# x plus attention output moved from VectorE in the attention loop to GpSimd in the dense loop, through stored parts

## The reference

```
x2  = x + tanh(g_xattn) * autocorrelation(layernorm(x), ctx, ctx)
n   = layernorm(x2)
out = x2 + tanh(g_ffn) * (n @ W_base.T + b_base + moe(n))
moe: h = n @ A_w (8 experts x 16), gate from softmax(n @ W_gate.T) - threshold, (h * gate) @ B_w * 2
```

## Time and profile before

| | |
|---|---|
| three runs | 3029.5, 3030.46, 3032.73 us; median 3030.46 us |
| profiled execution | 3031.29 us, its span 3029.5 us |
| mean granted clock of TensorE | 0.990 |
| PE busy | 2921.9 us, 96% |
| DVE, ACT, POOL busy | 1606.0, 1012.6, 1454.0 us |
| HBM read, written | 223.76 MB, 67.21 MB |

### The profile page before, as it was taken

How to read it: one execution, slowest core, us unless ns; L and a number is a source line. 1 busy time by engine, 2 the same in 40 slices (tenths; PEclk the granted TensorE clock), 3 DMA queues, 4 the chain that set the end, 5 groups by cost and what they waited for, 6 DMA issues and landing times.

```text
span 3029.5 us, 37059 instructions
## 1 busy us (share of the span) xinstructions
PE 2921.9 (96%) x13184; PEld 1466.0 (48%) x13184; DVE 1606.0 (53%) x2738; ACT 1012.6 (33%) x1672; POOL 1454.0 (48%) x577
## 2 busy tenths in 40 slices
PE   4999999999999999997799999999999999999999
PEld 2445554555545554553644444444444444444444
DVE  3899989999999999998722121121211112111111
ACT  4555556555555545441511121111211112111110
POOL 4788888889888888884031211212112121221210
PEclk8999999999999999999899999999999999999999
DMA  8455544555455554423634132331323313233230
GB/s 201 124 123 126 139 110 118 127 132 125 115 122 125 135 117 102 101 73 111 237 98 111 56 111 75 91 111 55 111 72 94 106 60 111 69 97 99 68 97 28
DMA packets 260355, 324.49 MB, mean 107 GB/s; under 512 B 162911, under 2 KB 163487, under 8 KB 245541
## 3 DMA queue, kind: packets, MB, share of 16 engines
q1 hardware_dynamic: 259922, 323.38, 40.1%
q10 hardware_dynamic: 348, 0.18, 0.0%
HBM read 223.76 MB, written 67.21 MB: 96 GB/s over the span
## 4 chain that ended last, share of the span: by engine, by line
PE 84%; DVE 5%; POOL 3%; issue 2%; DMA 2%; ACT 1%; SPq 1%; ACTq 0%; DVEq 0%; POOLq 0%
PE bank L1097 43%; PE bank L488 7%; PE bank L422 7%; PE bank L454 6%; PE bank L472 5%; PE bank L460 3%; POOL spec_o L869 3%; DVE rows_mem L1256 2%; PE bank L1086 1%; PE bank L1087 1%; PE bank L1088 1%; ACT wt L548 1%; PE bank L435 1%; PE bank L405 1%; PE bank L411 1%
## 5 line engine op out<-in xcount | busy, mean ns | idle before, releaser
L1281 POOL TENSOR_TENSOR rows_mem<-norm,rows_mem 128x2048 f16<-128x2048 f32 x31 | 126.1, 4068 | 1220.7 <-ACT rows_mem L1156 1220.7
L1097 PE MATMUL bank<-w_hi,rows_mem 128*128 128x512 f16 x2048 | 489.3, 379 | 3.8 <-DVE rows_mem L1256 3.8
L1097 PE MATMUL bank<-w_hi,xres_mem 128*128 128x512 f16 x2048 | 489.0, 379 | 3.5 <-DVE rows_mem L1256 3.5
L869 POOL TENSOR_TENSOR spec_o<-spec_o,term 128x1024 f32<-128x1024 f32 x190 | 443.3, 2362 | 40.6 <-DVE term L686 40.6
L1249 DVE TENSOR_TENSOR hwt_lo<-bank,hwt_hi 128x128 f16<-128x128 f32 x32 | 9.3, 292 | 790.4 <-ACT hwt_hi L1175 790.4
L1097 PEld LDWEIGHTS bank<-w_hi,rows_mem 128*128 128x128 f16 x2048 | 200.2, 98 | 251.6 <-DVE rows_mem L1256 13.6
L1097 PEld LDWEIGHTS bank<-w_hi,xres_mem 128*128 128x128 f16 x2048 | 200.2, 98 | 250.6 <-DVE rows_mem L1256 12.7
L488 PE MATMUL bank<-spec_o,table 128*128 128x512 f32 x512 | 249.1, 617 | 19.9 <-POOL spec_o L869 15.8
L1097 PE MATMUL bank<-w_lo,xres_mem 128*128 128x512 f16 x1024 | 262.8, 379 | 0.0
L1097 PE MATMUL bank<-w_lo,rows_mem 128*128 128x512 f16 x1024 | 262.8, 379 | 0.0
L422 PE MATMUL bank<-rows_mem,table 128*128 128x512 f32 x512 | 227.7, 598 | 18.0 <-POOL rows_mem L849 15.7
(11 more groups left out here) (182 smaller groups left out, 4876.3 us busy)
## 6 DMA issues: line engine op xcount, KB each, us to landing
rows_mem<-in_x_dram SPq DMA_DIRECT2D x32, 1024.0 KB, 13.0
norm<-x_scratch SPq DMA_DIRECT2D x32, 1024.0 KB, 5.5
rows_mem<-x_scratch SPq DMA_DIRECT2D x32, 1024.0 KB, 7.0
out_dram<-rows_mem SPq DMA_DIRECT2D x32, 1024.0 KB, 4.4
norm<-in_x_dram SPq DMA_DIRECT2D x28, 1024.0 KB, 10.8
rows_mem<-in_ctx_dram SPq DMA_DIRECT2D x256, 64.0 KB
rows_mem<-in_ctx_dram SPq DMA_DIRECT2D x64, 256.0 KB
xres_mem<-in_x_dram SPq DMA_DIRECT2D x256, 64.0 KB
```

Source lines behind the costliest of these rows:

```text
L869: pool.tensor_tensor(to, to, buffer, sign).then_inc(term_added, 1)
L1097: mm = pe.matmul(dense[o][:, :], nt(par, part)[:, k, :], w[:, k, o * 512:(o + 1) * 512], start=(k == 0 and n == 0), stop=False)
L1281: pool.tensor_tensor(norm_lo, norm[:, :], norm_hi, ALU.subtract).then_inc(norm_lo_made, 1)
```

## The change

The attention loop no longer forms x2. ACT copies `out_tiles`, scaled by tanh(g), into `kept` (`keep_out`, two operations of 128x1024 in a step), and SP stores this 1 MB twice: in natural row order (`parts_behind`, eight DMAs) and with the rows reversed (`parts_ahead`, four DMAs). The ten loads of `load_res` and DVE's `residual` are gone. POOL's `sum_qk` is gone too: DVE writes two of the four products into the PSUM banks of the spectra and does both sums. PE does `q_spectra(i+1)` at the end of step i, between the two halves of `out_tiles`.

In the dense layer ACT's queue loads natural rows of x into `norm` and the cosine part into `addend`; POOL adds them (`form`), ACT's queue loads the sine part, POOL adds or subtracts it, and ACT's queue stores the result as x2, from where SP loads `row` later. `addend` takes the place of the second `row` buffer, so SP loads row i+1 once out i is stored. A tile is formed two tiles ahead, and its statistics, normalisation and rounding move from two tiles ahead to one. The first tile is formed by POOL at step 31, from loads that SP issues in step 30.

The core of the diff:

```diff
+    x2_rows = nc.dram_tensor("x2_scratch", (ROWS, 128, D), f32, kind="Internal").ap()
+    parts = [nc.dram_tensor(n, (2 * B, 2, 128, D), f32, kind="Internal").ap() for n in ("parts_ahead", "parts_behind")]
+    parts_ahead = parts[0].rearrange("k a (n p) c -> k a n p c", p=16)[:, :, :, ::-1, :]
...
+                def store(i):
+                    sp.wait_ge(out_kept, 2 * (i + 1))
...
+                    for n in range(8):
+                        sp.dma_start(parts[1][2 * b:2 * b + 2, :, 112 - 16 * n:128 - 16 * n, c:c + C].rearrange("h a p c -> p (h a) c"),
+                                     kept[16 * n:16 * n + 16].rearrange("p h a c -> p (h a) c")).then_inc(parts_stored, 16)
                     for h in range(2):
+                        for a in range(2):
+                            sp.dma_start(parts_ahead[2 * b + h, a, :, :, c:c + C], kept[:, h, a, :]).then_inc(parts_stored, 16)
...
-                    if i < STEPS:
-                        load_res(i, par)
...
+                    if i == STEPS - 2:
+                        first_tile()
                     if i == STEPS - 1:
-                        first_norm()
+                        sp.wait_ge(formed, 2)
+                        sp.dma_start(x2_rows[0], norm[:, :]).then_inc(x2_kept, 16)
                         for m in range(4):
                             early_weights(m)
...
-                            pe.wait_ge(sine_added, 4 * (c - 1) + 2 * (y + 1))
+                            pe.wait_ge(out_kept, 2 * (c - 1) + y + 1)
...
-                    pe.wait_ge(prod_made, 2 * (i + 1))
+                    pe.wait_ge(q_used, 2 * (i + 1))
...
-                    if most(i) < STEPS:
-                        q_spectra(i, mine)
...
+                    if most(i) + 1 < STEPS:
+                        q_spectra(i + 1, other)
+                    if least(i) >= 1:
                         out_tiles(i - 1, (phase - 1) % NCH, mine, 0)
...
+                def keep_out(c, four, h):
+                    if h == 1 and least(c) >= 1:
+                        act.wait_ge(parts_stored, 192 * c)
+                    act.wait_ge(out_made, 2 * c + 2 - h)
+                    act.activation(kept[:, h, :, :], pair(four, 1 - h), ACT.Copy, scale=gates[:, 0:1]).then_inc(out_kept, 1)
...
+                    if least(i) >= 1:
+                        keep_out(i - 1, mine, 1)
                     if most(i) < STEPS:
                         scale_w(i)
+                    if least(i) >= 1:
+                        keep_out(i - 1, mine, 0)
...
-                    dve.tensor_tensor(prod_b[:, 0:2, :], imag, k[:, 3:5, :], ALU.mult)
-                    dve.tensor_tensor(prod_a[:, 2:4, :], imag, k[:, 0:3:2, :], ALU.mult).then_inc(q_used, 1)
+                    dve.tensor_tensor(real, imag, k[:, 3:5, :], ALU.mult).then_inc(qk_made, 1)
+                    dve.tensor_tensor(imag, imag, k[:, 0:3:2, :], ALU.mult).then_inc(qk_made, 1)
+                    dve.wait_ge(qk_made, 4 * i + 3)
+                    dve.tensor_tensor(prod_a[:, 0:2, :], real, prod_a[:, 0:2, :], ALU.add).then_inc(q_used, 1)
+                    dve.wait_ge(qk_made, 4 * i + 4)
+                    dve.tensor_tensor(prod_a[:, 2:4, :], imag, prod_b[:, 2:4, :], ALU.subtract).then_inc(q_used, 1)
...
-                    if least(i) >= 1:
-                        residual(i - 1, 1 - par, mine)
...
-                    if most(i) < STEPS:
-                        sum_qk(i)
...
-                    pe.wait_ge(sine_added, 4 * STEPS)
+                    pe.wait_ge(out_kept, 2 * STEPS)
...
+                def load_norm(i):
+                    if fleast(i) == 1:
+                        act.wait_ge(wt_made, 2 * JOBS)
+                        load_cosine(i, 1)
+                    else:
+                        act.wait_ge(norm_hi_made, i - 1)
+                        act.wait_ge(norm_lo_made, i - 1)
+                    act.nop(nofuse=True)
+                    act.dma_start(norm[:, :], x_rows[i]).then_inc(norm_loaded, 16)
+                def load_sine(i, par):
+                    act.wait_ge(formed, 2 * i + 1)
...
+                    act.dma_start(addend, parts[par][i // 2, 1]).then_inc(sine_loaded, 16)
+                def keep_x2(i, par):
+                    act.wait_ge(formed, 2 * (i + 1))
...
+                    act.dma_start(x2_rows[i], norm[:, :]).then_inc(x2_kept, 16)
+                    if fmost(i) + 1 < ROWS:
+                        load_cosine(i + 1, 1 - par)
                 def step(i, par):
                     gating(i)
+                    if fmost(i) + 1 < ROWS:
+                        deviation_rows(act, i + 1)
+                        normalise_rows(act, i + 1)
+                        rounded(i + 1, 1 - par)
                     if fmost(i) + 2 < ROWS:
-                        normalise(i + 2)
-                        rounded(i + 2, par)
-                    hw_hi(i)
+                        load_norm(i + 2)
+                        if fleast(i) == 0:
+                            hw_hi(i)
+                        load_sine(i + 2, par)
+                        keep_x2(i + 2, par)
+                    if fleast(i) >= 1:
+                        hw_hi(i)
-                weights_hi(0, 2)
-                normalise(0)
-                weights_hi(2, 2 * JOBS)
-                normalise(1)
-                rounded(1, 1)
+                weights_hi(0, 2 * JOBS)
+                load_norm(1)
+                load_sine(1, 1)
+                keep_x2(1, 1)
                 tiles(act, step)
...
+                def form(i, par):
+                    pool.wait_ge(norm_loaded, 32 * i)
+                    pool.tensor_tensor(norm[:, :], norm[:, :], addend, ALU.add).then_inc(formed, 1)
+                    pool.wait_ge(sine_loaded, 16 * i)
+                    pool.tensor_tensor(norm[:, :], norm[:, :], addend, (ALU.subtract, ALU.add)[par]).then_inc(formed, 1)
                 def step(i, par):
-                    pool.wait_ge(x2_loaded[par], 16 * (i // 2 + 1))
-                    pool.tensor_tensor(row[:, par, :], row[:, par, :], bias[:, :], ALU.add).then_inc(bias_added, 1)
-                    if fmost(i) + 2 < ROWS:
-                        remainder(i + 2, par)
+                    if fmost(i) + 1 < ROWS:
+                        remainder(i + 1, 1 - par)
+                    pool.wait_ge(x2_loaded, 16 * (i + 1))
+                    pool.tensor_tensor(row, row, bias[:, :], ALU.add).then_inc(bias_added, 1)
+                    if fmost(i) + 2 < ROWS:
+                        form(i + 2, par)
```

More of the change, by code:

```diff
@@ L496, in tensor_attention @@
                 v_spectra(0, 0, X(0))
+                q_spectra(0, X(0))
                 pe.wait_ge(ident_loaded, 16)
@@ L936, in weight_row @@
             def weight_row(n):
-                m = n - 1
-                return (row if m % 4 < 2 else wrow)[:, m % 2, :]
+                return rows_mem[:, (n - 1) % 4, :]
             def weight_target(n, h, part):
```

183 lines of the change are left out of this document (79 added, 104 removed).

## The result

| | before | after |
|---|---|---|
| median of 8 runs each | 3030.31 us | 3022.39 us (3019.65 to 3023.82) |
| ratio, 95% interval | | 0.9974 (0.9965 to 0.9982) |
| profiled execution, span | 3031.29, 3029.5 us | 3023.82, 3022.0 us |
| mean granted clock | 0.990 | 0.994 |
| HBM read, written | 223.76, 67.21 MB | 257.32, 134.32 MB |

The account below looks back on a forecast made before the run. PE's own order was taken as the bound, so only PE's waits count: -1 - 6.5 - 6 + 0 + 6.5 = -7 us, from 3031.3 to 3024.3, less 0.8 to the median: 3023.5 us; 8-in-10 range 3010 to 3046.

Parts of the forecast that it names:

- The attention loop: Some 30 steps: POOL's wait in out_tiles goes, -3 us; new wait for ACT's copy, +2; sum -1 us (-7 to +28).
- Rival (b): Attention loop: ACT's copy lies open in each step, +29 us, giving 3051 us; chance 0.08.
- whichever holds, they are hidden: Attention loop: DVE's two added sums, taken at 1.22 us, are hidden because correlate comes over 12 us later.
- The first two steps: Attention start: correlate(0) 2 us earlier, step 1's loss of about 4.5 us gone; -6.5 us (-9 to -2).
- From attention to weights: Between the stages: stores issued earlier, W_base loads begin 7.4 us earlier, 1.5 us given back; -6 us (-10 to 0).
- The dense loop: Steady dense tiles: ACT is at hw_hi before turn_hw, so forming x2 costs nothing; 0 us (0 to +20).
- The ring: Dense tile's chain from experts through gating, statistics, x loads and POOL sums to hw_hi; delays experts once 5.1 us longer.
- Rival (a): Dense loop: the ring becomes the bound, 0.6 to 0.7 us of stall a tile, first tiles 16 more; 3060 us; chance 0.13.
- The first tiles: Dense start without lead: logits(1) just in time, experts(1) at 1605.7 where due at 1599.2; +6.5 us (0 to +18).
- Rival (c): Lower clock and DVE's pace hide half the gains of the first two steps and attention to weights; 3030 us; chance 0.16.
- Rival (d): First dense tiles lose little, each load taking 5.5 us: 6 us less, 3017.5 us; chance 0.14.
- Rival (e): First dense tiles: POOL and DVE meet and block each other, three times 4 us; 3035.5 us; chance 0.04.

Follow-up runs that it names:

- q_back: Kernel after, but q_spectra(i) again at the start of PE's step i: 3075.81 us, ratio 1.0152 against before.
- q_back_pool: Kernel after, with q_spectra(i) again at the start of PE's step and POOL again summing q times k: 3027.2 us, 0.9989 against before.
- pool_sums: Kernel after, but POOL again sums the products of q and k, q_spectra staying early: 3025.11 us, 0.9986 against before.
- weights_between: Kernel after, but W_base blocks 4 to 7 are loaded between the natural and reversed stores of step 31: 3021.8 us, 0.9972 against before.
- ring_9: Kernel after, with POOL's first sum of each dense tile taken back and redone over all 2048 columns (added work): 3185.21 us, 1.0511 against before.
- gate_row0: Kernel after, with gating(0) ahead of x(1)'s sine part and SP's row 0 held until x(1) and its cosine part landed: 3017.9 us, 0.9961 against before.
- best: Kernel after with the edits of gate_row0 and weights_between together: 3018.14 us, 0.9958 against before.

## Why the prediction was right, point by point

**The attention loop** (-1, measured +0.7). The mechanism was right, but both sizes were off, and with them the sign: the loop lost a little where it was to gain. POOL's wait was worth 2.1 us and not 3, the wait for ACT's copy 3.9 us and not 2; `w_spectra`, for which nothing was forecast, took 1.2 us less. The forecast took `w_spectra` 2.30 us behind `turn_w`, which is what it is; but against 2.22, the one row that it read, where the mean of before is 63.16 / 29 = 2.18. And ACT's copy took 1.12 us against 0.97. Rival (b), the copy lying open, has fallen.

Left unasked was something behind the sentence "whichever holds, they are hidden", on DVE's sums. It holds, and for the reason given, the early `q_spectra(i+1)`. But it asked only when `correlate` needs the sums, over 12 us later, and not when they let go of the PSUM banks in which the change keeps the products, which `w_spectra` needs 2.3 us behind `turn_w`. q_back shows the price of that, 52 us over the loop, and q_back_pool its cause. In after the first sum ends at 1319.19 and `w_spectra` starts at 1321.75: this, 2.6 us, is the cover, not 12. It is also why both expectations for q_back were wrong by 50 us.

**The first two steps** (-6.5, measured -6.6). pool_sums bears out the part at the start: 2.7 us by the medians, 3.2 by the mean starts of `correlate(0)` (59.9 and 56.6 us), for the 2 us taken. In step 1 the stall is gone, but the three reasons named are not one sum: the sums on DVE and the place of `q_spectra` are each enough alone, and the ten loads have no part in it, for q_back_pool, which lacks them, waits as before does.

**From attention to weights** (-6, measured -8.0). The loads of W_base began 7.3 us earlier, 7.4 was forecast. The weights were done 6.7 us earlier. The other 1.3 us are `logits(0)`, 2.92 us instead of 4.23, and that is luck: of the twelve traces with the change it took 2.92 us in eight and 4.2 to 4.5 us in four. PE's waits in weights_between are for the blocks of this stream up to its end, as was taken.

**The dense loop** (0, measured 0). The ring costs nothing and has 5.75 us of room where the forecast had 5.1. Rival (a) needed 5.1 us more and has fallen; its turning point is about where it was put. Its price beyond that point was too low, since it counted the wait alone: ring_9 paid 4.4 us a tile for 3.4 us of excess.

**The first tiles** (+6.5, measured +6.4). The size is right in this trace, and the place is wrong. Forecast were a stall ahead of `experts(1)` and transposes of tile 1 "just in time". Everything from `base(0)` on lay 13.9 us earlier than in the forecast's times; against that, x(1) was issued only 13.2 us earlier and landed 2.6 us later than taken (11.1 for 8.5 us), the remainder ended 2.4 us later, and the transposes took 7.7 us instead of 5.5 behind it. So the transposes came 4.5 us late, PE lost 6.1 us there, and the chain behind, which was to be 6.5 us late one tile later, met a PE that was as late itself: `hw_hi(1)` at 1590.79, forecast 1605.0 - 13.9 = 1591.1, and 0.3 us of stall. One lateness shows once, at the first place that meets it. The working has a slip of 0.4 us besides: 1501.4 + 8.5 + 14.5 and two issues of 0.4 are 1525.2, not 1525.6.

That the size came out as +6.4 is in part luck, and it hangs on `logits(0)`. Six traces have the code of after in the first tiles. In the four in which `logits(0)` took 2.92 us, the stall at `logits(1)` was 3.2 to 4.8 us and `base(0)` to `base(3)` 146.7 to 149.0. In the two in which it took 4.4 and 4.5 us (weights_between and q_back_pool), `base(0)` came later, the stall was 1.8 and 2.0 us, and the three tiles took 145.3 and 145.4 us. The gain of the row above and the loss of this one thus belong together. Their sum, forecast at +0.5, was -1.6 in after and between -4.5 and 0 in the other five.

**The sum** (3023.5 us, measured 3022.4) is better than its parts: the loop came out 1.7 us too slow and the stretch before `base(0)` 2.0 us too fast. Rival (c), gains hidden by the clock and by DVE, has fallen with the 6.6 and 8.0 us of the two parts that it would have halved. Rival (d), small losses in the first tiles, is half borne out by the two traces with 145.3 and 145.4 us.

**Rival (e)**, POOL and DVE meeting in the first tiles, did not happen in after. The sum of two single columns, whose long case stood in the earlier trace rows, has this group in after, by line and shape over the dense layer:

```profile
L1262 DVE TENSOR_TENSOR wsum<-wsum,wzero 128x1 f32<-128x1 f32 x32 | 5.1, 159 | 1.1
```

159 ns in the mean of 32, where one case of 4.02 us had made the mean of before 280 ns. ACT starts no gating before the second sum is done, and this order keeps the two engines apart. Where gating(0) comes first they do meet. In gate_row0 it runs beside POOL's first sum of tile 1 (L1315, up to 1499.67), and one operation on eight columns, with its two scalars in SBUF as well, lasts up to the end of that sum:

```profile
1496.09 3.61 DVE L1261 TENSOR_SCALAR gate<-gate,erec,thr 128x8 f32<-128x8 f32 x1
```

Its median in the other tiles is 0.29 us; in best it took 2.25 us. Neither cost anything, for the first tiles of both took 142.1 us. The rule of the Trainium skill (SBUF — State Buffer, Who interferes with whom) fits both catches: a DVE instruction with two inputs in SBUF contends with a GpSimd one that reads SBUF.

## What to carry to other kernels

When a product is kept in the PSUM bank that it was read from, the bank is free only after the sum that reads it again; ask who writes that bank next before asking when the sum is done. When work goes from a full engine to an idle one and the period is PE's, look for the gain in the fill, the drain and the first iterations, and put the order of the DMAs there by hand: 1 MB fewer in flight ahead of the first tile was worth 4 us here. To learn how near a ring is to becoming the bound, put a known delay into it twice, once below and once above the room that you expect.

## What the runs showed of the hardware beyond what was expected

- 1 MB of x in whole rows landed after 5.7 us in the steady state of the dense layer, after 6.8 to 7.1 us as the second of two MB (three traces) and after 9.6 to 11.2 us as the last of three, on two queues (nine traces; 11.1 in after).
- With the DMA engines full, between the stages, a 1 MB block of W_base landed every 2.5 us, and moving four of them ahead of the reversed stores moved the landing of the last by 0.8 us.
- In after the DMA transpose of the rounded half of tile 1 landed 4.4 us after its issue. That of the remainder, beside the load of x(2) (both issued at 1531.62), landed after 7.5 us, and the load after 5.6; the DMA share was 0.94 from 1535 to 1539.
- An operation of DVE on 128x8 with three operands in SBUF took 3.61 us in gate_row0 and 2.25 us in best, in both up to the end of a sum on POOL, and 0.29 us elsewhere.
- A stall can cost more than its length: behind 4.5 us of it the granted clock was 0.66 for a stretch of 5 us, and `logits(1)` took 4.52 us instead of 2.92, a third more on top of the stall. Behind stalls of 1.8 and 2.0 us (weights_between, q_back_pool) it took the usual 2.92.
